# Layer attention: other places among the eight periods of a step for the small operations of each sequence, with queries and keys still evacuated by two VectorE instructions

## The chip, the cores and the metric

The kernel runs as one program on one core of a Trainium2 chip. The metric is the device time of an execution in microseconds (us); the times below are of three executions and of one more that was profiled. Everything is float32 (some operands are read as fp32r, the same bits).

## The reference

The input is 16 sequences of 256 tokens with 128 features. The program computes a four-layer network, a mixture of experts, a second attention and the mixture of experts again. The change is in the attention of the four layers, `_attn`:

```python
for l in range(L):                       # L = 4
    m = _mamba(x, ...)
    x = _ln(x + m, g1[l], be1[l])
    a = _attn(x, W_qkv[l], b_qkv[l], W_ao[l], b_ao[l])
    x = _ln(x + a, g2[l], be2[l])
    h = gelu(x @ W_f1[l].T + b_f1[l]); x = x + h @ W_f2[l].T + b_f2[l]

def _attn(x, W_qkv, b_qkv, W_ao, b_ao):  # 16 heads of 8, per sequence of 256 tokens
    q, k, v = split(x @ W_qkv.T + b_qkv)
    scores = einsum('bhqd,bhkd->bhqk', q, k) * SCALE
    wts = softmax(scores, axis=-1)
    o = einsum('bhqk,bhkd->bhqd', wts, v)
    return o @ W_ao.T + b_ao
```

## The kernel before

Each engine runs its own stream of instructions, written out by hand; semaphores order them. The layer attention (`head_attention`, one function for each engine) is a pipeline over the 16 sequences, a **step** for each: `heads` calls `step(b, r)` for b = 0 to 15 on every engine (r = b mod 4 picks one of four buffers `hqk` and `hvx`). A step has eight **periods** p = 0 to 7, called p0 to p7 here. B counts sequences over all layers. `nth(s, B)` is the count of semaphore s when the work for B is done.

What a period holds on TensorE (`step`, L892):

- rows: scores with the query on the partition, for two heads of a *later* sequence (b+1 in p0 to p3, b+2 in p4 to p7), into PSUM banks 0 and 1 (`row`, L829). They serve only to find each row's maximum. In an even period VectorE reduces both banks in one instruction (`two_maxima`, L1883). In an odd one it reduces bank 0 (`maxima`, L1876), while ScalarE copies bank 1 out (`copy_row`, L1489), which VectorE then reduces from SBUF (`copied_maxima`, L1892). The rows of the next period wait until banks 0 and 1 are free (`freed`).
- scores: with the key on the partition, for two heads of b, into two of the banks 2 to 5 (`score`, L848). ScalarE takes the exponential of both heads in one instruction of 128x1024 (`exps`, L1468).

Around them stand the small operations, once for each sequence. All but `values` and `raw` (bank 6) go through PSUM bank 7, one after another:

- `project_v` (L822), copied out by `lay_v` on VectorE (L1906). Its input is a copy of x that GpSimd makes (`copy_x`, L2331).
- `project_qk` (L816, L817), evacuated by `evac_qk` on VectorE, two instructions (L1900). GpSimd splits the result in two parts (`parts`, L2338 to L2343), SyncE writes it to HBM (`spill`, L579) and reads it back spread over the partitions (`scatter`, L588).
- the maxima of b+1: GpSimd splits them (`split_max`, L2360), TensorE transposes them (`maxima`, L870), ScalarE copies them out (`max_rows`, L1461), and SyncE sends them by two DMAs into two partitions of each head's block of `hqk` (`send_max`, L595), where the scores of step b+1 pick them up. So TensorE's first wait in a step is `pe.wait_ge(hd_mx, every(hd_mx, B))`.
- `values(b, j)` (L861): weights times v for a quarter j of the heads; ScalarE copies the sum out after the last quarter (`raw`, L1474).
- `sums(b)` (L877) spreads the softmax sums; ScalarE makes their reciprocal by Ln and Exp (`reciprocal`, L1480 and L1482), GpSimd multiplies (`divide`, L2350), `out` (L883) projects, and `add_out` on VectorE (L1913) adds to x.

Before the change the small operations of step b stand so. TensorE: p0 `project_v(b+1)`, p1 `values(b-1, 3)`, p2 `project_qk(b+3)`, p3 `values(b, 0)`, p4 `sums(b-1)`, p5 `values(b, 1)` then the transposes of b+1, p6 `values(b, 2)`, p7 `out(b-1)`. Bank 7 has one user at a time, so each of them waits for the one before to have been read out: `sums(b-1)` in p4 waits for hd_q, the end of `evac_qk(b+3)`, which VectorE does at the end of p3.

The loop `heads` runs step 0, three rounds of four steps, and steps 13 to 15 apart, which leave out what has no later sequence (n1, n2, n3: whether b+1, b+2, b+3 exist).

## Time and profile before

| | |
|---|---|
| three executions | 2674.94, 2678.55, 2682.89 us; median 2678.55 |
| the profiled execution | 2679.11 us, of which 2677.4 us from its first to its last instruction |
| TensorE's mean granted clock | 0.908 of full speed |
| busy, share of the span | TensorE 80%, VectorE 62%, ScalarE 60%, GpSimd 26% |
| attention of layer 0, step 0 to the last `values` | 173.0 to 416.0 us; it occurs four times |
| chain that ended last, largest parts | TensorE L829 8%, VectorE L1883 6%, DMA hqk<-hmt 3% |

A busy share is a mean over stages with different limits. The chain that ended last follows the program back from its last instruction, at each step to what released it. "DMA hqk<-hmt" is the sending of the maxima. In the rows, the third number from the end of a stretch is the granted clock of TensorE (1.00 is 2.4 GHz, 0.50 is 1.2 GHz).

### The profile page before, as it was taken

Reading aid. Unit: us, or ns where it says so; the run is one execution under the profiler, and the core shown is the slowest. Engines: PE = TensorE matmul, PEld = TensorE weight load, DVE = VectorE, ACT = ScalarE, POOL = GpSimd, SP = SyncE. Lnnn points to the kernel's source line nnn. Section 1 sums busy time; section 2 is a strip of 40 time slices with the busy share of each in tenths; the row PEclk is TensorE's granted clock in tenths of the full one; section 3 lists DMA queues with packets and bytes.
Section 4 is the critical chain, followed back from the end, with each engine's and each line's share of the span. In section 5 each row is a group of like instructions: output and inputs, shape, how many; then the busy total and the mean of one; then the engine's idle time right before and its main releaser. Section 6 shows DMA issues by size and latency. Waiting matters only on the chain.

```text
span 2677.4 us, 49462 instructions
## 1 busy us (share of the span) xinstructions
PE 2136.1 (80%) x15147; PEld 1401.1 (52%) x15147; DVE 1664.4 (62%) x2491; ACT 1618.9 (60%) x2604; POOL 700.9 (26%) x980
## 2 busy tenths in 40 slices
PE   6968889987888896888899688887877478886795
PEld 4534445643444663444475344454666347775584
DVE  4557775656775765777475577756643267767541
ACT  6447778745777763777784477886544214454461
POOL 0113221022231102223101233211757130004664
PEclk8969999996999997899999699998988789997897
DMA  3033320013331002333000333204141201004223
GB/s 114 10 96 107 110 74 7 9 45 92 110 100 50 16 0 81 94 100 108 20 9 10 96 97 112 81 7 88 46 118 53 70 0 32 1 9 93 79 90 128
DMA packets 116930, 171.73 MB, mean 64 GB/s; under 512 B 13728, under 2 KB 75168, under 8 KB 116512
## 3 DMA queue, kind: packets, MB, share of 16 engines
q1 hardware_dynamic: 107552, 150.66, 19.9%
q0 software_dynamic: 9216, 19.02, 2.0%
q8 instruction: 88, 1.44, 0.2%
q14 instruction: 74, 0.61, 0.1%
HBM read 85.19 MB, written 82.35 MB: 63 GB/s over the span
## 4 chain that ended last, share of the span: by engine, by line
PE 49%; DVE 14%; POOL 11%; issue 10%; DMA 6%; ACT 6%; SPq 1%; DVEq 1%; ACTq 0%; POOLq 0%
PE ps L829 8%; DVE hmx L1883 6%; POOL back_scratch L2420 6%; PE ps L861 5%; POOL slot_scratch L2415 5%; DMA hqk<-hmt 3%; PE ps L877 2%; ACT hrow L1489 2%; PE ps L762 2%; PE ps L726 2%; PE ps L732 2%; PE ps L677 2%; PE ps L683 2%; PE ps L1257 1%; PE ps L1149 1%
## 5 line engine op out<-in xcount | busy, mean ns | idle before, releaser
L1468 ACT ACTIVATE hpt<-ps 128x1024 f32<-128x1024 f32 x512 | 518.5, 1020 | 57.3 <-PE ps L848 56.8
L829 PE MATMUL ps<-hqk 24*128 24x256 f32 x2048 | 287.1, 361 | 154.9 <-DVE hmx L1883 92.0
L829 PEld LDWEIGHTS ps<-hqk 24*128 24x128 f32 x2048 | 173.3, 208 | 368.3 <-DVE hmx L1883 207.6
L1883 DVE TENSOR_REDUCE hmx<-ps 128x4 f32<-128x1024 f32 x256 | 312.8, 1222 | 62.2 <-PE ps L829 60.0
L861 PE MATMUL ps<-hpt,hvx 128*32 128x256 f32 x4096 | 296.2, 410 | 21.8 <-ACT hpt L1468 21.2
L1876 DVE TENSOR_REDUCE hmx<-ps 128x2 f32<-128x512 f32 x256 | 177.3, 693 | 158.9 <-PE ps L829 158.9
L848 PE MATMUL ps<-hqk 26*128 26x256 f32 x2048 | 271.0, 346 | 2.8 <-ACT hpt L1468 1.6
L1489 ACT ACTIVATE hrow<-ps 128x512 f32<-128x512 f32 x256 | 151.9, 593 | 188.1 <-PE ps L829 188.1
L1892 DVE TENSOR_REDUCE hmx<-hrow 128x2 f32<-128x512 f32 x256 | 176.1, 688 | 40.1 <-ACT hrow L1489 29.9
L2420 POOL DMA_INDIRECT back_scratch<-ys,xslot x160 | 153.2, 958 | 86.8 <-issue 47.9
L848 PEld LDWEIGHTS ps<-hqk 26*128 26x128 f32 x2048 | 161.9, 196 | 22.3 <-ACT hpt L1468 16.5
L861 PEld LDWEIGHTS ps<-hpt,hvx 128*32 128x32 f32 x4096 | 111.8, 114 | 115.2 <-ACT hpt L1468 35.0
L2415 POOL DMA_INDIRECT slot_scratch<-xtok,slot_i x128 | 131.6, 1028 | 62.4 <-issue 38.4
L2360 POOL CAST hhl<-hmx 128x32 fp32r<-128x32 f32 x64 | 13.4, 209 | 404.6 <-DVE hmx L1892 404.6
L2312 POOL MEMSET hqk<- 128x1024 f32 x16 | 14.5, 952 | 390.1 <-PE ps L732 390.1
L1740 DVE TENSOR_TENSOR unit<-ps,rstd 128x512 f32<-128x512 f32 x64 | 44.2, 690 | 104.0 <-ACT rstd L1372 103.2
L2350 POOL TENSOR_TENSOR hon<-hraw,hrec 128x512 f32<-128x512 f32 x64 | 81.4, 1271 | 93.3 <-ACT hrec L1482 93.3
L877 PE MATMUL ps<-hraw,spread 128*128 128x512 f32 x128 | 74.1, 662 | 39.3 <-DVE hqk L1900 39.3
L677 PE MATMUL ps<-streams,center 128*128 128x512 f32 (+1 forms) x192 | 96.0, 623 | 9.4 <-SPq L549 5.1
L2331 POOL COPY hxs<-streams 128x256 f32 (+1 forms) x64 | 25.4, 396 | 298.0 <-PE ps L822 273.2
L1439 ACT ACTIVATE hidh<-ps,mw 128x512 fp32r<-128x512 f32 x128 | 89.4, 698 | 19.9 <-PE ps L789 19.9
L683 PE MATMUL ps<-sq,average 128*128 128x512 f32 x192 | 96.4, 601 | 3.6 <-ACT sq L1358 3.3
(326 smaller groups left out, 5342.9 us busy)
## 6 DMA issues: line engine op xcount, KB each, us to landing
hqk_scratch<-hqks SPq DMA_DIRECT2D x64, 768.0 KB, 3.2
hqk<-hqk_scratch SPq DMA_DIRECT2D x256, 192.0 KB
slot_scratch<-filler SPq DMA_DIRECT2D x10, 1040.0 KB, 15.7
xslot<-slot_scratch SPq DMA_DIRECT2D x20, 520.0 KB, 4.2
yback<-back_scratch SPq DMA_DIRECT2D x32, 256.0 KB, 4.4
mw<-mw_in SPq DMA_DIRECT2D x10, 516.5 KB, 3.5
w12raw<-w_in SPq DMA_DIRECT2D x1, 2560.0 KB, 9.3
back_scratch<-ys,xslot POOLq DMA_INDIRECT x160, 2.2
```

What stands on the lines that cost most here:

```text
L677: mm(ps[:, k, :], center[:], src[:, ds(c * CH, CH)], start=True, stop=True).then_inc(ln_cen, 1)
L683: mm(ps[:, 4 + k % 2, :], average[:], sq[:, k % 2, :], start=True, stop=True).then_inc(ln_var, 1)
L829: return mm(ps[:, o % 2, qt * SEQ:(qt + 1) * SEQ], hqk[r][32 * g:32 * g + 24, j, 0, qt * P:(qt + 1) * P], hqk[r][32 * g:32 * g + 24, j, 1, ...
L848: return mm(ps[:, 2 + g, kt * SEQ:(kt + 1) * SEQ], hqk[r][32 * g:32 * g + 26, j, 1, kt * P:(kt + 1) * P], hqk[r][32 * g:32 * g + 26, j, 0, ...
L861: last = mm(ps[32 * g:32 * g + 32, 6, (j // 2) * SEQ:(j // 2 + 1) * SEQ], hvx[r][:, kt, g, j, :], hpt[:, j, g, kt, :], start=j % 2 + kt == ...
L1468: A(hpt[:, j, g:g + 2, :, :], ps[:, 2 + g:4 + g, :], ACT.Exp, scale=QSCALE).then_inc(hd_exp, 1)
L1489: A(hrow[:, o // 4 % 2].rearrange("p t k -> p (t k)"), ps[:, 1, :], ACT.Copy).then_inc(hd_max[1], 1)
L1876: V.tensor_reduce(hmx[:, r, :, 4 * g + j], ps[:, o % 2, :].rearrange("p (t k) -> p t k", t=2), AX.X, ALU.max).then_inc(hd_max[0], 1)
L1883: V.tensor_reduce(hmx[:, r].rearrange("p t (g j) -> p g t j", j=4)[:, g:g + 2, :, j], ps[:, bank:bank + 2, :].rearrange("p x (t k) -> p x ...
L1892: V.tensor_reduce(hmx[:, r, :, 4 * g + j], hrow[:, o // 4 % 2], AX.X, ALU.max).then_inc(hd_red, 1)
L2415: G_.indirect_dma_start(slot_d, bass.IndirectOffsetOnAxis(slot_i[:, c, t:t + 1], 0), xtok[c][:, t, :], None).then_inc(sent, 16)
L2420: G_.indirect_dma_start(back_d, bass.IndirectOffsetOnAxis(xslot[:, g * 4 + b, D:D + 1].bitcast(I32), 0), ys[:, g % 4, b, :], None).then_in ...
```

## The change

The small operations get other periods. On TensorE: p0 `project_qk(b+3)`, p1 `values(b-1, 3)`, p2 `out(b-2)`, p3 `values(b, 0)`, p4 `sums(b-1)`, p5 the transposes of b+1 then `values(b, 1)`, p6 `project_v(b+1)`, p7 `values(b, 2)`. The waits for bank 7 follow the new order. `out` and `divide` now run a step later (b-2 in place of b-1), so the last two steps hold two of them, and steps 0 and 1 none. VectorE evacuates, lays out and adds in the periods of its producers (p0, p6, p2). ScalarE copies the maxima (`max_rows`) ahead of the exponentials of p5 instead of behind them, and its reciprocal is in two parts: Ln behind the exponentials of p4 (`logarithm`), Exp behind those of p7. GpSimd's order in a step is `divide`, `parts`, `split_max`, `copy_x` in place of `copy_x`, `split_max`, `parts`, `divide`. SyncE's order is as before. The loop has two rounds of four steps, with the others written out. No instruction of a whole step is added or taken away.

```diff
--- before.py
+++ after.py
@@ -526,10 +526,14 @@
 
         def heads(eng, step, last):
 
-            step(0, 0, first=True)
-            with eng.Fori(0, 3) as i:
+            step(0, 0, first=True, second=True)
+            step(1, 1, second=True)
+            with eng.Fori(0, 2) as i:
                 for k in range(4):
-                    step(i * 4 + (1 + k), (1 + k) % 4)
+                    step(i * 4 + (2 + k), (2 + k) % 4)
+            step(10, 2)
+            step(11, 3)
+            step(12, 0)
             step(13, 1, n3=False)
             step(14, 2, n2=False, n3=False)
             step(15, 3, n1=False, n2=False, n3=False)
@@ -595,7 +599,7 @@
                         sp.dma_start(hqk[r][24 + part:P:32, :, 0].bitcast(F32),
                                      hmt[16 * part:16 * part + 16].bitcast(F32)).then_inc(hd_mx, 16)
 
-                def step(b, r, first=False, n1=True, n2=True, n3=True):
+                def step(b, r, first=False, second=False, n1=True, n2=True, n3=True):
                     if n3:
                         spill(b + 3)
                     if n1:
@@ -889,7 +893,7 @@
                         last = mm(ps[:, 7, 0:1], T("wo", x * D, D), T("bv", x, 1), start=x == 0, stop=x == 1)
                     last.then_inc(hd_bp, 1)
 
-                def step(b, r, first=False, n1=True, n2=True, n3=True):
+                def step(b, r, first=False, second=False, n1=True, n2=True, n3=True):
                     B = l * BATCH + b
                     for p in range(8):
                         if p == 0:
@@ -911,41 +915,44 @@
                             last = score(2 * p + 1, r, t)
                         last.then_inc(hd_sc, 1)
 
-                        if p == 0 and n1:
-                            pe.wait_ge(hd_mt, nth(hd_mt, B))
-                            pe.wait_ge(hd_ao, nth(hd_ao, B - 2))
-                            project_v(b + 1)
+                        if p == 0 and n3:
+                            if first:
+                                pe.wait_ge(hd_mt, nth(hd_mt, B))
+                            else:
+                                pe.wait_ge(hd_v, nth(hd_v, B))
+                            project_qk(b + 3)
                         if p == 1 and not first:
                             values(b - 1, 3, (r + 3) % 4)
-                        if p == 2 and n3:
-                            pe.wait_ge(hd_v, nth(hd_v, B + 1))
-                            project_qk(b + 3)
+                        if p == 2 and not second:
+                            if n3:
+                                pe.wait_ge(hd_q, nth(hd_q, B + 3, 1))
+                            else:
+                                pe.wait_ge(hd_v, nth(hd_v, B))
+                            out(b - 2)
                         if p == 3:
                             values(b, 0, r)
                         if p == 4 and not first:
-                            if n3:
+                            if second:
                                 pe.wait_ge(hd_q, nth(hd_q, B + 3, 1))
-                            elif n1:
-                                pe.wait_ge(hd_v, nth(hd_v, B + 1))
                             else:
                                 pe.wait_ge(hd_ao, nth(hd_ao, B - 2))
                             sums(b - 1)
                         if p == 5:
-                            values(b, 1, r)
                             if n1:
                                 if first:
                                     pe.wait_ge(hd_q, nth(hd_q, B + 3, 1))
                                 else:
                                     pe.wait_ge(hd_ln, nth(hd_ln, B - 1))
                                 maxima(b + 1)
-                        if p == 6:
+                            values(b, 1, r)
+                        if p == 6 and n1:
+                            pe.wait_ge(hd_mt, nth(hd_mt, B + 1))
+                            project_v(b + 1)
+                        if p == 7:
                             values(b, 2, r)
-                        if p == 7 and not first:
-                            if n1:
-                                pe.wait_ge(hd_mt, nth(hd_mt, B + 1))
-                            else:
+                            if not n1:
                                 pe.wait_ge(hd_ln, nth(hd_ln, B - 1))
-                            out(b - 1)
+                                out(b - 1)
 
                 def last():
                     values(15, 3, 3)
@@ -1473,11 +1480,14 @@
                     act.wait_ge(hd_on, nth(hd_on, B - 1))
                     A(hraw[:].rearrange("p x n -> p (x n)"), ps[:, 6, :], ACT.Copy).then_inc(hd_raw, 1)
 
-                def reciprocal(b):
+                def logarithm(b):
                     B = l * BATCH + b
                     act.wait_ge(hd_sel, nth(hd_sel, B))
                     act.wait_ge(hd_on, nth(hd_on, B - 1))
                     A(hrec[:].rearrange("p x n -> p (x n)"), ps[:, 7, :], ACT.Ln).then_inc(hd_ln, 1)
+
+                def reciprocal(b):
+                    B = l * BATCH + b
                     act.wait_ge(hd_ln, nth(hd_ln, B))
                     A(hrec[:], hrec[:], ACT.Exp, scale=-1.0).then_inc(hd_rec, 1)
 
@@ -1488,18 +1498,22 @@
                     act.wait_ge(hd_red, nth(hd_red, B, o // 4 - 2))
                     A(hrow[:, o // 4 % 2].rearrange("p t k -> p (t k)"), ps[:, 1, :], ACT.Copy).then_inc(hd_max[1], 1)
 
-                def step(b, r, first=False, n1=True, n2=True, n3=True):
+                def step(b, r, first=False, second=False, n1=True, n2=True, n3=True):
                     for p in range(8):
                         ahead, o = (1, 8 + 2 * p) if p < 4 else (2, 2 * p - 8)
                         if p % 2 == 1 and (n1 if p < 4 else n2):
                             copy_row(b + ahead, o + 1)
+                        if p == 5 and n1:
+                            max_rows(b + 1)
                         exps(b, p)
                         if p == 1 and not first:
                             raw(b - 1)
                         if p == 4 and not first:
+                            logarithm(b - 1)
+                            if not n1:
+                                reciprocal(b - 1)
+                        if p == 7 and not first and n1:
                             reciprocal(b - 1)
-                        if p == 5 and n1:
-                            max_rows(b + 1)
 
                 def first_v():
                     act.wait_ge(pool_step, cleared(l))
@@ -1507,8 +1521,12 @@
 
                 if part == "begin":
                     return [lambda: evac_qk(0), first_v, lambda: evac_qk(1)]
+                def last_reciprocal():
+                    logarithm(15)
+                    reciprocal(15)
+
                 if part == "end":
-                    return [lambda: reciprocal(15)]
+                    return [last_reciprocal]
 
                 evac_qk(2)
                 copy_row(0, 3)
@@ -1913,7 +1931,7 @@
                     V.scalar_tensor_tensor(xa[:, ds(b * SEQ, SEQ)], ps[:, 7, 0:SEQ], hbo[:],
                                            xa[:, ds(b * SEQ, SEQ)], ALU.add, ALU.add).then_inc(hd_ao, 1)
 
-                def step(b, r, first=False, n1=True, n2=True, n3=True):
+                def step(b, r, first=False, second=False, n1=True, n2=True, n3=True):
                     for p in range(8):
                         ahead, o, ra = (1, 8 + 2 * p, (r + 1) % 4) if p < 4 else (2, 2 * p - 8, (r + 2) % 4)
                         if n1 if p < 4 else n2:
@@ -1922,11 +1940,13 @@
                             else:
                                 maxima(b + ahead, o, ra)
                                 copied_maxima(b + ahead, o + 1, ra)
-                        if p == 0 and n1:
+                        if p == 0 and n3:
+                            evac_qk(b + 3)
+                        if p == 2 and not second:
+                            add_out(b - 2)
+                        if p == 6 and n1:
                             lay_v(b + 1, (r + 1) % 4)
-                        if p == 3 and n3:
-                            evac_qk(b + 3)
-                        if p == 7 and not first:
+                        if p == 7 and not n1:
                             add_out(b - 1)
 
                 if part == "end":
@@ -2362,14 +2382,16 @@
                     G_.tensor_tensor(hhl[:, :, 1, :], hmx[:, r], hhl[:, :, 0, :].bitcast(F32), ALU.subtract)\
                       .then_inc(hd_mlo, 1)
 
-                def step(b, r, first=False, n1=True, n2=True, n3=True):
+                def step(b, r, first=False, second=False, n1=True, n2=True, n3=True):
+                    if not second:
+                        divide(b - 2)
+                    if n3:
+                        parts(b + 3)
+                    if n1:
+                        split_max(b + 1, (r + 1) % 4)
                     if n2:
                         copy_x(b + 2)
-                    if n1:
-                        split_max(b + 1, (r + 1) % 4)
-                    if n3:
-                        parts(b + 3)
-                    if not first:
+                    if not n1:
                         divide(b - 1)
 
                 pool.wait_ge(ln_aff, nth(ln_aff, l * (2 * NC)))
```

How the instructions stand now. TensorE, from the rows and scores of p4 to those of p6 in a step inside the loop (829/833 rows, 848/852 scores, 877/881 `sums`, 861/865 `values`, 870/874 transposes; the second number of each is the line after the change). Before:

```order
L877 MATMUL ps<-hraw,spread 128x512
L835 REGISTER_ALU
L829 MATMUL ps<-hqk_161 128x256 x2
L848 MATMUL ps<-hqk_163 128x256 x2
L829 MATMUL ps<-hqk_161 128x256 x2
L848 MATMUL ps<-hqk_163 128x256 x2
L861 MATMUL ps<-hpt,hvx_167 32x256 x8
L870 MATMUL ps<-ident,hhl 32x128 x2
```

The same place after:

```order
L881 MATMUL ps<-hraw,spread 128x512
L839 REGISTER_ALU
L833 MATMUL ps<-hqk_161 128x256 x2
L852 MATMUL ps<-hqk_163 128x256 x2
L833 MATMUL ps<-hqk_161 128x256 x2
L852 MATMUL ps<-hqk_163 128x256 x2
L872 REGISTER_ALU
L874 MATMUL ps<-ident,hhl 32x128 x2
L865 MATMUL ps<-hpt,hvx_167 32x256 x8
```

The transposes have moved from behind the matmuls of `values(b, 1)` to ahead of them.

ScalarE, from the exponentials of p4 to those of p6 (1468/1475 exponentials, 1480/1487 Ln, 1482/1492 Exp of the reciprocal, 1489/1499 `copy_row`, 1461/1468 `max_rows`). Before:

```order
L1468 ACTIVATE hpt<-ps 128x1024
L1478 REGISTER_ALU
L1480 ACTIVATE hrec<-ps 128x512
L1482 ACTIVATE hrec<-hrec 128x512
L1487 ISA
L1488 ISA
L1489 ACTIVATE hrow<-ps 128x512
L1466 REGISTER_ALU
L1468 ACTIVATE hpt<-ps 128x1024
L1459 REGISTER_ALU
L1460 ISA
L1461 ACTIVATE hmt<-ps 32x256
```

The same place after:

```order
L1475 ACTIVATE hpt<-ps 128x1024
L1485 REGISTER_ALU
L1487 ACTIVATE hrec<-ps 128x512
L1497 ISA
L1498 ISA
L1499 ACTIVATE hrow<-ps 128x512
L1466 REGISTER_ALU
L1467 ISA
L1468 ACTIVATE hmt<-ps 32x256
L1473 REGISTER_ALU
L1475 ACTIVATE hpt<-ps 128x1024
```

The Exp of the reciprocal has left this place, and `max_rows` stands ahead of the exponentials of p5.

VectorE, from the maxima of p3 to those of p4 (1892/1910 `copied_maxima`, 1883/1901 `two_maxima`, 1900/1918 `evac_qk`). Before:

```order
L1892 TENSOR_REDUCE hmx<-hrow 128x2
L1897 ISA
L1898 REGISTER_ALU
L1900 TENSOR_SCALAR hqk_169<-ps,tw 128x256 x2
L1882 ISA
L1883 TENSOR_REDUCE hmx<-ps 128x2x2
```

After, where the two evacuations stand now, between the maxima of p0 and those of p1 (1894 is `maxima`):

```order
L1901 TENSOR_REDUCE hmx<-ps 128x2x2
L1915 ISA
L1916 REGISTER_ALU
L1918 TENSOR_SCALAR hqk_169<-ps,tw 128x256 x2
L1893 REGISTER_ALU
L1894 TENSOR_REDUCE hmx<-ps 128x2
```

The pair of evacuations has moved from ahead of the `two_maxima` of p4 to ahead of the `maxima` of p1.

## Rows read from the trace of the kernel before

**Rows 1.** Stretches: length, busy us of PE, PEld, DVE, ACT, POOL, clock, DMA

```profile
173.03:191.67 18.64, 15.41 (x122) 8.06 (x123) 11.54 (x16) 9.71 (x13) 3.43 (x7) 0.50 0.17 61
314.25:330.42 16.17, 13.57 (x146) 7.18 (x146) 11.67 (x17) 11.88 (x17) 4.68 (x8) 0.89 0.33 99
345.30:360.19 14.89, 12.12 (x145) 6.39 (x145) 11.75 (x17) 11.73 (x17) 4.67 (x8) 1.00 0.36 108
316.00:318.00 2.00, 1.90 (x24) 0.81 (x24) 1.68 (x4) 1.25 (x2) 0.06 (x1) 0.71 0.80 169
1658.00:1660.00 2.00, 2.00 (x26) 0.84 (x24) 1.38 (x2) 1.57 (x3) 0.00 (x0) 0.57 0.81 169
```

**Rows 2.** Timeline of TensorE in one step: start us, us, [idle before <-releaser]

```profile
345.30 0.38 PE L829 MATMUL ps<-hqk 24*128 24x256 f32 x2 [0.51 <-DMA hqk<-hmt]
...
345.74 0.71 PE L822 MATMUL ps<-tw,hxs 128*128 128x128 f32 x4
347.15 0.38 PE L829 MATMUL ps<-hqk 24*128 24x256 f32 x2 [0.69 <-DVE hmx L1883]
...
348.58 0.38 PE L829 MATMUL ps<-hqk 24*128 24x256 f32 x2
...
350.43 0.38 PE L829 MATMUL ps<-hqk 24*128 24x256 f32 x2 [0.28 <-DVE hmx L1883]
...
351.87 0.38 PE L829 MATMUL ps<-hqk 24*128 24x256 f32 x2
...
353.23 1.12 PE L877 MATMUL ps<-hraw,spread 128*128 128x512 f32 x2 [0.86 <-DVE hqk L1900]
354.36 0.39 PE L829 MATMUL ps<-hqk 24*128 24x256 f32 x2
...
355.81 0.39 PE L870 MATMUL ps<-ident,hhl 128*32 128x128 f32 x2
356.19 0.38 PE L829 MATMUL ps<-hqk 24*128 24x256 f32 x2
...
357.11 1.07 PE L861 MATMUL ps<-hpt,hvx 128*32 128x256 f32 x16 [0.41 <-ACT hpt L1468]
358.11 0.38 PE L829 MATMUL ps<-hqk 24*128 24x256 f32 x2
...
358.54 1.13 PE L883 MATMUL ps<-hon,tw 128*128 128x256 f32 x4
```

**Rows 3.** Timeline of VectorE in the same step

```profile
345.87 1.23 DVE L1883 TENSOR_REDUCE hmx<-ps 128x4 f32<-128x1024 f32 x1 [0.29 <-PE ps L829]
347.01 0.41 DVE L1906 COPY hvx<-ps 128x256 f32<-128x256 f32 x1
...
352.31 0.87 DVE L1900 TENSOR_SCALAR hqk<-ps,tw 128x256 f32<-128x256 f32 x2
353.09 1.22 DVE L1883 TENSOR_REDUCE hmx<-ps 128x4 f32<-128x1024 f32 x1
```

**Rows 4.** Timeline of ScalarE in the same step

```profile
347.79 0.60 ACT L1489 ACTIVATE hrow<-ps 128x512 f32<-128x512 f32 x1 [0.78 <-PE ps L829]
...
354.39 0.60 ACT L1480 ACTIVATE hrec<-ps 128x512 f32<-128x512 f32 x1 [0.82 <-PE ps L877]
355.02 0.63 ACT L1482 ACTIVATE hrec<-hrec 128x512 f32<-128x512 f32 x1
...
356.94 0.36 ACT L1461 ACTIVATE hmt<-ps 32x256 fp32r<-32x256 f32 x1
```

**Rows 5.** Timeline of GpSimd in the same step

```profile
353.44 0.61 POOL L2338 CAST hqks<-hqk 128x512 fp32r<-128x512 f32 x1 [0.35 <-DVE hqk L1900]
...
356.06 1.27 POOL L2350 TENSOR_TENSOR hon<-hraw,hrec 128x512 f32<-128x512 f32 x1
```

**Rows 6.** The chain that ended last, between two steps: start us, us, what

```profile
357.32 0.55 SPq L595
...
357.91 1.97 DMA hqk<-hmt
```

## The prediction

> **What bounds the kernel now.** I read the list of waits first, then the chain that ended last, then one step of layer 0 on each engine, and last the granted clock of several stretches. In the steps at full clock no engine is full: of 14.89 us TensorE is busy 12.12, VectorE 11.75, ScalarE 11.73 [rows 1]. The step is held by a chain that goes to and fro. TensorE writes rows, VectorE or ScalarE must empty banks 0 and 1, and only then may the next rows come. The reader is to see in the timeline how long each period lasts, from one row of L829 to the next [rows 2]: p0 1.85, p1 1.43, p2 1.85, p3 1.44, p4 2.49, p5 1.83, p6 1.92, and p7 to the end of the step at 360.19 [rows 1] 2.08 us.
>
> Two of these lengths are natural. In an even period VectorE starts its double reduction 0.57 after the rows (345.87 against 345.30), it takes 1.23 [rows 3], and TensorE goes on about 0.05 later: 1.85. TensorE's own work fits under it: rows and scores take 0.44 (345.30 to 345.74), and the `project_qk` of p2 ended 0.28 before p3 began, so at 1.57 [rows 2]. In an odd period with `values` TensorE is busy throughout: 0.44 and about 1.0, that is 1.43. The copy by ScalarE there starts at 0.64 and ends at 1.24 [rows 4], so it is hidden.
>
> The rest is stall, at three places [rows 2]. In p4 `sums` stood idle 0.86 for the evacuation of queries and keys, and it ended only at 354.35: 2.49 in place of 1.85. In p6 `values(b, 2)` waited 0.41 for exponentials that ScalarE did late, since Ln and Exp stood ahead of them [rows 4]: 1.92 in place of 1.85. In p7 `out` takes no longer than `values`, but the next step waited 0.51 for the maxima to arrive (the bracket of the first row shows this at the start of this step): 2.08 in place of 1.43.
>
> **The change, part by part.**
>
> *Evacuation out of p3.* The two instructions hold VectorE 0.78 (352.31 to 353.09) ahead of p4's double reduction [rows 3]. In the new order p4's `sums` waits for `add_out(b-2)` of p2, which is long over. It starts at 0.44 and ends at 1.57, under the 1.85 of the period. Gain 2.49 - 1.85 = 0.64.
>
> *Evacuation into p0.* `project_qk` there ends at 1.57. VectorE is free for its next instruction 1.14 after the start of its reduction (347.01 against 345.87), at 0.57 + 1.14 = 1.71. The pair occupies it to 2.49. The rows of p1, which starts at 1.85, are ready for VectorE some 0.53 later, at 2.38: the `maxima` of p1 starts 0.11 late, at 2.49, and with 0.69 (an estimate: somewhat over half of the double reduction's 1.22) ends at 3.18. TensorE is held by `values` until 1.85 + 1.43 = 3.28. Cost nothing, with 0.05 to 0.1 to spare. This is the tightest place, and the one where two instructions in place of one would show. If the cover is gone, each 0.1 of lateness costs 0.1 a step.
>
> *Maxima earlier.* Now the transposes are issued at 0.44 of p5 and take 0.38 (355.81 to 356.19). ScalarE copies bank 1 at 0.64, is free again 0.48 later, and does `max_rows` from about 1.12 to 1.48 of p5. Before, it ended at 357.30, which is 2.94 into p5. Behind it stay the same two issues, one of 0.55, and the transfer of 1.97 [rows 6]: from 357.30 to TensorE's start at 360.19 are 2.89. So the maxima arrive at 1.48 + 2.89 = 4.37 after the start of p5. The step ends at 1.83 + 1.85 + 1.43 = 5.11. The wait is gone with 0.74 to spare. Gain in p7 2.08 - 1.43 = 0.65. What is behind `send_max` on SyncE's queue, `scatter(b+3)`, starts earlier too and harms nothing. `spill(b+3)`, ahead of it, hangs on `parts`, which start some 3 us into the step and last 2.62 (353.44 to 356.06) [rows 5]: done near 5.5, long before `send_max` at about 10.
>
> *Ln in p4, Exp behind p7.* `sums` ends at 1.57, Ln takes 0.60 [rows 4], so it ends at about 2.2 of p4; the transposes need bank 7 at 1.85 + 0.44 = 2.29. It fits by less than 0.1. Behind the transposes on TensorE `values(b, 1)` and all rows of p6 are queued, so lateness here would be paid in full. The exponentials of p5 start at 1.38 of p5 and end at 2.4; their user `values(b, 2)` now stands in p7, at 1.83 + 1.85 + 0.44 = 4.12. The wait in p6 is gone. p6 has `project_v`, 0.71 [rows 2], under VectorE's 1.85: gain 1.92 - 1.85 = 0.07. The Exp (0.63) follows p7's exponentials and pushes those of the next p0 by 0.4, to end near 2.2; ScalarE's next work, the copy of p1, comes at 1.85 + 0.64 = 2.49. GpSimd's `divide`, 1.27 [rows 5], ends near 2.5 of the next step, and `raw` in p1 needs it at 3.9, `out(b-2)` in p2 at 3.28 + 0.44 = 3.72. Here 1.2 are to spare. The ends of Exp, raw and `divide` are late next, but nobody waits.
>
> *Order of the same instructions:* p5 keeps 1.83, whichever of transposes and `values` is first. More written-out steps in place of a round of the loop: I take nothing, as no back-jump shows as a stall in TensorE's timeline.
>
> **The sum.** A whole step at full clock becomes 4 x 1.85 + 3 x 1.43 + 1.83 = 13.52, against 14.89: 1.36 less (0.64 + 0.65 + 0.07). Steps 2 to 12 of a layer have this, 11 x 1.36 = 15.0. Step 0 runs at half clock, 18.64 [rows 1], where TensorE is the bound nearly throughout; the same matmuls in another order give nothing. Step 1 comes to full clock in its middle: 0.9, an estimate from p4 to p7. Step 13 has no `project_qk`, so no wait in p4 to lose: 0.72. At the end an `out` and a `divide` more in step 15, where ScalarE's exponentials are the bound: I take a loss of 0.2 (bounds +0.2 and -1.1, a full `out`). Together 15.0 + 0.9 + 0.72 - 0.2 = 16.4 a layer, 65.7 for four.
>
> *The clock.* A step in which the clock falls lasts 16.17, 1.28 more [rows 1]. I counted eight short falls in steps 2 to 12 of the four layers, from the one at 316 to the one at 1658 [rows 1], each just behind the thin stretch of p7 and p0, where TensorE stands still twice. These gaps are filled now (`project_qk` in p0), and the thinnest place is p6. The Trainium skill, TensorE: Matmul & The Clock Gate, Part 1, says that activity releases the clock and idleness takes it back; by it, with no long idleness in a step, there would be no falls, before or after, and nothing to gain: 2613. The trace does not agree: it has falls with TensorE never idle longer than 0.9 in the step. I take half of the eight falls away: 4 x 1.28 = 5.1. The bounds are all eight (10.2) and eight more (-10.2).
>
> The sum against the profiled execution's own 2679.11: 2679.1 - 65.7 - 5.1 = 2608. The median of the runs, 2678.55, is 0.02% away, so it holds for the median as well.
>
> **The rivals.**
> (a) Part of the stall comes back at a tight place: Ln to transposes, or evacuation to `maxima` of p1, each with 0.1 or less to spare. With 0.5 a step given back (half an exponential on ScalarE), 52 steps x 0.5 = 26: 2634. For it: both margins are as small as the 0.1 to which I can read starts. Against it: what I used are gaps between starts in the same step. Chance 0.17.
> (b) The clock falls no longer: 2603. Denser work in p7 and p0 speaks for it, falls of unclear origin against. Chance 0.2; it lies in the likeliest one's range.
> (c) Slower: the clock. At half clock a step takes 18.6 or more [rows 1], 5.1 above the new 13.52, since TensorE has nothing to hide it under. The gain of 1.36 is used up when TensorE is at half clock for 1.36/5.1 = 27% of steps 1 to 12; before, the eight falls cost 8 x 1.28, as much as 2.7 steps of the 44 at half clock (each 18.64 - 14.89 = 3.75), 6%. If the half clock of step 0 and 1 lasted five steps longer in each layer, 20 x 5.1 - 65 = +37: 2716. Nothing in the order asks for it; the pattern of the first two steps is only slightly changed. Chance 0.04.
> (d) The change does not do what it says, as another wait takes the whole 1.36: a late Ln by 1.4 would, and so would `send_max` held back behind `spill` by over 0.74 + 1.4. Then 2679. Chance 0.03.
>
> **How the numbers follow.** The forecast has 0.56, with (b) as its lower edge 0.76: 2596 to 2625. (a) reaches to 2645. I give 2592 to 2640. A measurement of this kernel can tell about 0.3% (8 us) from no change. Forecast, (b) and (a) are faster by more than that: 0.93; within it (d) and little of (c): 0.035; slower 0.035.
>
> **What would show it.** In the changed kernel's trace: a step of 13.5 at full clock; no wait of L833 for DMA hqk<-hmt and none of `sums` for the evacuation; `max_rows` starting within 1.2 of p5's rows; even periods of 1.85 and odd ones of 1.43; `maxima` of p1 starting about 0.1 behind its rows. Steps 14 and 15 unchanged in length to 0.5. The prediction is wrong if even periods are longer than 1.9 (VectorE late), if the transposes wait for Ln, or if the mean granted clock falls below 0.88.

## The result

The changed kernel takes 2605.3 us (median of four, 2592.7 to 2607.8), the kernel before 2680.7 in the same comparison (2674.9 to 2686.4). The ratio is 0.971, with a 95% interval of 0.967 to 0.975. Forecast were 2608 us and a range of 2592 to 2640.

| | before | after |
|---|---|---|
| the profiled execution, its span | 2679.1, 2677.4 | 2607.8, 2606.1 |
| a steady step at full clock | 14.88 | 13.53 |
| 11 steps, from `sums(1)` to `sums(12)`, four layers | 665.3 | 595.0 |
| steps among them in which the clock fell, apart from a fall that begins in the last 0.7 | 8 | 0 |
| from the first scores of a layer to `sums(1)`, four layers | 175.2 | 167.0 |
| from `sums(12)` to `sums(15)`, four layers | 144.5 | 146.4 |
| TensorE's mean granted clock | 0.908 | 0.906 |

The span is 71.3 shorter, and the eleven steady steps of four layers hold 70.3 of it. These are the stretches of the four layers before and after, from the view of chosen stretches; the columns are as in [rows 1]. Before:

```profile
217.17:382.39 165.22, 134.08 (x1580) 70.51 (x1581) 128.52 (x174) 128.62 (x176) 50.95 (x86) 0.99 0.36 108
664.43:832.06 167.63, 136.83 (x1580) 71.75 (x1580) 128.23 (x174) 128.68 (x176) 50.94 (x86) 0.97 0.36 106
...
sum 665.34, PE 541.37 PEld 284.33 DVE 513.24 ACT 514.31 POOL 203.73; mean PE 135.34 PEld 71.08 DVE 128.31 ACT 128.58 POOL 50.93
```

And after, the same view:

```profile
217.13:365.89 148.76, 130.71 (x1584) 69.48 (x1580) 129.22 (x175) 128.05 (x177) 49.37 (x84) 1.00 0.40 118
645.66:794.41 148.75, 130.70 (x1584) 69.48 (x1580) 129.21 (x175) 128.04 (x177) 49.33 (x84) 1.00 0.40 118
...
sum 595.01, PE 522.85 PEld 277.96 DVE 516.87 ACT 512.18 POOL 197.39; mean PE 130.71 PEld 69.49 DVE 129.22 ACT 128.05 POOL 49.35
```

The reader is to see that the busy time of VectorE and ScalarE hardly changed. What went is mostly TensorE's waiting (665.3 less 541.4 busy before, 595.0 less 522.9 after, so 124 against 72), and the clock is 1.00 in every layer. Of the 70.3, 44 x (14.88 - 13.52) = 59.8 are shorter steps, and 10.5 the falls of the clock that no longer occur. (14.88 stands for the usual step; at full clock single ones of the 44 took 13.97 to 15.60 before, and 13.48 to 13.54 after.) The mean clock of the whole execution is no higher for it: the stretches at half clock outside these steps stay, in a shorter execution, and two falls are new there (below).

One step after the change on TensorE, from its timeline, which answers to [rows 2]. It begins at 304.79; the rows above that are p5, p6 and p7 of the step before it.

```profile
299.70 0.39 PE L833 MATMUL ps<-hqk 24*128 24x256 f32 x2 [0.28 <-DVE hmx L1901]
...
300.18 0.39 PE L874 MATMUL ps<-ident,hhl 128*32 128x128 f32 x2
300.50 1.07 PE L865 MATMUL ps<-hpt,hvx 128*32 128x256 f32 x16
301.50 0.38 PE L833 MATMUL ps<-hqk 24*128 24x256 f32 x2
...
303.35 0.38 PE L833 MATMUL ps<-hqk 24*128 24x256 f32 x2 [0.70 <-DVE hmx L1901]
...
304.79 0.38 PE L833 MATMUL ps<-hqk 24*128 24x256 f32 x2
...
306.64 0.39 PE L833 MATMUL ps<-hqk 24*128 24x256 f32 x2 [0.28 <-DVE hmx L1901]
...
308.10 0.39 PE L833 MATMUL ps<-hqk 24*128 24x256 f32 x2
...
309.95 0.38 PE L833 MATMUL ps<-hqk 24*128 24x256 f32 x2 [0.28 <-DVE hmx L1901]
...
311.39 0.38 PE L833 MATMUL ps<-hqk 24*128 24x256 f32 x2
```

The periods last: p5 1.80, p6 1.85, p7 1.44, p0 1.85, p1 1.46, p2 1.85, p3 1.44. Every idle time left is VectorE's double reduction, in an even period. No row of the step waits for a DMA or for `evac_qk`. VectorE's timeline of the same stretch, which answers to [rows 3]:

```profile
305.36 1.23 DVE L1901 TENSOR_REDUCE hmx<-ps 128x4 f32<-128x1024 f32 x1
306.50 0.87 DVE L1918 TENSOR_SCALAR hqk<-ps,tw 128x256 f32<-128x256 f32 x2
307.29 0.68 DVE L1894 TENSOR_REDUCE hmx<-ps 128x2 f32<-128x512 f32 x1
```

ScalarE's, which answers to [rows 4]:

```profile
300.36 0.60 ACT L1499 ACTIVATE hrow<-ps 128x512 f32<-128x512 f32 x1 [0.30 <-PE ps L833]
300.85 0.36 ACT L1468 ACTIVATE hmt<-ps 32x256 fp32r<-32x256 f32 x1
```

And SyncE's queue, which answers to [rows 6]:

```profile
301.23 1.11 SPq L599 DMA_DIRECT2D hqk<-hmt  x2
302.57 1.55 SPq L592 DMA_DIRECT2D hqk<-hqk_scratch  x4
310.42 0.35 SPq L583 DMA_DIRECT2D hqk_scratch<-hqks  x1
```

The evacuation starts 1.71 into the step and the `maxima` of p1 2.50, as worked out (1.71, 2.49). `max_rows` starts 1.15 into p5 and ends at 1.51 (1.12, 1.48). The spill is issued 5.6 into the step. The maxima are issued 4.3 behind the spill of their own step, at 301.23 in a step that began 13.53 before 304.79, so 10.0 into it.

### The profile page after: what moved, and what is told of

Read it like the earlier page. It is cut to its first block, busy times and chain, and to the rows that moved or that the text cites. A ratio compares the mean times of both kernels' runs of the same rounds, so it can differ in the third digit from the quotient of the medians.

```text
span 2606.1 us, 49174 instructions
## 1 busy us (share of the span) xinstructions
PE 2120.5 (81%) x15147; PEld 1396.0 (54%) x15147; DVE 1667.8 (64%) x2491; ACT 1613.6 (62%) x2604; POOL 703.9 (27%) x980
## 4 chain that ended last, share of the span: by engine, by line
PE 57%; DVE 18%; POOL 10%; issue 8%; ACT 3%; DMA 3%; DVEq 1%; SPq 1%; ACTq 0%; POOLq 0%
DVE hmx L1901 12%; PE ps L833 11%; PE ps L865 10%; POOL slot_scratch L2437 5%; POOL back_scratch L2442 4%; PE ps L766 2%; PE ps L730 2%; PE ps L736 2%; PE ps L681 2%; PE ps L687 2%; PE ps L1264 1%; PE ps L1241 1%; PE ps L1156 1%; PE ps L1189 1%; PE ps L791 1%
## 5 line engine op out<-in xcount | busy, mean ns | idle before, releaser
L865 PE MATMUL ps<-hpt,hvx 128*32 128x256 f32 x4096 | 290.3, 403 | 0.0
L1910 DVE TENSOR_REDUCE hmx<-hrow 128x2 f32<-128x512 f32 x256 | 176.0, 688 | 10.5
L1866 DVE TENSOR_TENSOR hidl<-hid,hidh 128x1024 fp32r<-128x1024 f32 x64 | 78.4, 1224 | 31.5 <-ACT hid L1447 30.0
L1374 ACT ACTIVATE logv<-ps,acol 128x512 f32<-128x512 f32 x96 | 65.8, 685 | 52.8 <-PE ps L687 52.4
L2351 POOL COPY hxs<-streams 128x256 f32<-128x256 f32 (+1 forms) x64 | 25.5, 398 | 252.3 <-PE ps L826 227.5
## 6 DMA issues: line engine op xcount, KB each, us to landing
slot_scratch<-filler SPq DMA_DIRECT2D x10, 1040.0 KB, 15.6
```

Source lines behind the costliest of these rows:

```text
L865: last = mm(ps[32 * g:32 * g + 32, 6, (j // 2) * SEQ:(j // 2 + 1) * SEQ], hvx[r][:, kt, g, j, :], hpt[:, j, g, kt, :], start=j % 2 + kt == ...
L1910: V.tensor_reduce(hmx[:, r, :, 4 * g + j], hrow[:, o // 4 % 2], AX.X, ALU.max).then_inc(hd_red, 1)
```

## The experiments

Step lengths are intervals between the `sums` of two sequences, read from each kernel's timeline. "b" stands for the kernel before with an edit, "a" for the changed kernel with an edit. The first four kernels ran on a chip on which the kernel before takes 2859 us, 180 more. The kernel before has no profile there, but the four have: from `sums(15)` of layer 4 to the end of the program they take 1091 to 1098, the kernels of the other chips 915 to 919. So the extra time lies behind the attention of the layers, ratios are a little diluted by it, and I go by step lengths and by the 44 steady steps as well. These are the 44 steady steps of each profiled execution:

| kernel | usual step at full clock | the 44 steps | of them with a fall of the clock |
|---|---|---|---|
| before | 14.89 | 665.3 | 8 |
| b_fill | 14.89 | 655.1 | 0 |
| b_max | 14.89 | 655.1 | 2 |
| b_evac | 14.65 | 689.0 | 24 |
| b_both | 14.67 | 672.2 | 15 |
| changed, changed again | 13.53 | 595.0, 595.1 | 0, 0 |
| a_undo3 | 13.85 | 614.8 | 3 |
| a_parts | 14.67 | 733.6 | 38 |
| a_parts_sp | 15.02 | 696.6 | 27 |
| a_evac4 | 13.78 | 614.2 | 3 |
| a_evac1 | 13.52 | 594.7 | 0 |
| a_rec | 13.53 | 596.9 | 1 |
| a_split | 13.21 | 587.8 | 3 |

### Evacuation alone: b_evac

```diff
-                        if p == 3 and n3:
+                        if p == 2 and n3:
                             evac_qk(b + 3)
```

> The kernel before with one edit: VectorE evacuates queries and keys at the end of p2, right behind its double reduction, in place of the end of p3. Theory of three separate stalls: the wait of sums in p4 goes, p4 falls from 2.49 to 1.85 us, a step from 14.89 to 14.25, 12 steps in each of 4 layers: 31 us less than before (2648). The pair ends 0.1 late for the maxima of p3, hidden under values. Rival, one chain through the arrival of the maxima: the maxima of the next sequence arrive later relative to the step and p7 grows by as much as p4 loses, 2679. Second rival, that the gain comes mostly from the clock falling less often: step lengths at full clock unchanged.

Measured 2888.9 against 2859.1: ratio 1.0125 (1.009 to 1.016), slower. Single steps at full clock take mostly 14.4 to 14.9, usually 14.65: 0.24 less than before, where 0.64 was forecast. What makes the kernel slower is the clock: the 44 steady steps took 689.0, with mean clocks of 0.87 to 0.97 in the four layers. p4 lost its wait as expected (its `sums` start behind the scores at once), but p7 grew. SyncE's timeline between two steps:

```profile
298.98 0.35 SPq L579 DMA_DIRECT2D hqk_scratch<-hqks  x1
299.43 1.67 SPq L595 DMA_DIRECT2D hqk<-hmt  x2
```

ScalarE's, the copy that makes the maxima ready:

```profile
299.05 0.36 ACT L1461 ACTIVATE hmt<-ps 32x256 fp32r<-32x256 f32 x1
```

The chain, with the transfer of the maxima:

```profile
300.02 2.61 DMA hqk<-hmt
```

And TensorE's timeline, the matmul that waits for it:

```profile
302.94 0.38 PE L829 MATMUL ps<-hqk 24*128 24x256 f32 x2 [1.01 <-DMA hqk<-hmt]
```

The maxima were ready at 299.41, 0.43 behind the start of the spill's issue. The two issues took 1.67 in place of 1.11 and the transfer 2.61 in place of 1.97 [rows 6]. The wait at the end of p7 doubled. The size of the spill, from the page of the kernel before, with the number of transfers, their size and the time from issue to landing:

```profile
hqk_scratch<-hqks SPq DMA_DIRECT2D x64, 768.0 KB, 3.2
```

My theory of separate stalls fell here. The first rival had the mechanism, a chain through the arrival of the maxima, but p7 grew by less than p4 lost.

### Maxima alone: b_max, and both: b_both

```diff
                         if p == 5:
-                            values(b, 1, r)
                             if n1:
                                 ...
                                 maxima(b + 1)
+                            values(b, 1, r)
```

```diff
+                        if p == 5 and n1:
+                            max_rows(b + 1)
                         exps(b, p)
                         ...
-                        if p == 5 and n1:
-                            max_rows(b + 1)
```

> The kernel before with the transposes of p5 ahead of values(b, 1) on TensorE, and max_rows ahead of the exponentials of p5 on ScalarE. Theory: the maxima leave about 0.9 us earlier, the wait of 0.5 for their arrival goes. But the exponentials of p5 are 0.26 later and values(b, 2) in p6 waits for them longer, so the step falls by only 0.38, from 14.89 to 14.5: 20 us less (2660). Rival, that the arrival is the only thing that holds p6 to p0: a step falls by 0.65, 34 us less (2646).

Measured ratio 0.996 (0.9945 to 0.998). Steady steps take 14.8 to 15.1, as before; on the mean of the 44 a step is 0.05 shorter, and not 0.38. Most of the 7.5 us gained is the clock: 2 of the 44 steps have a fall, where the profile of the kernel before, on another chip, has 8. The transposes, now first, waited for Ln (0.18), which still stood behind `sums` held up by the evacuation, and the sending ran into the spill. TensorE's timeline:

```profile
293.89 0.39 PE L870 MATMUL ps<-ident,hhl 128*32 128x128 f32 x2 [0.18 <-ACT hrec L1480]
```

SyncE's timeline:

```profile
295.06 0.35 SPq L579 DMA_DIRECT2D hqk_scratch<-hqks  x1
295.45 1.71 SPq L595 DMA_DIRECT2D hqk<-hmt  x2
```

> The two edits together: evacuation behind the double reduction of p2, and transposes and max_rows first in p5. Theory of separate stalls: the gains add up, step 13.87 (14.89 - 0.64 - 0.38), 51 us less than before (2628), which leaves 0.35 a step to the changed kernel, for values(b, 2) waiting in p6. Rival, one chain: together no more than the larger of the two.

Measured ratio 1.0035 (1.0015 to 1.0054), steps at full clock mostly 14.2 to 14.8, the 44 steps 672.2. The maxima were ready at 294.24, but SyncE sends in order: the spill went out at 294.72 and they at 295.11, and their transfer took 2.67. The gains do not add up. In the kernel before, these two edits bring nothing while the spill keeps its place; the two with an earlier spill were not tried.

### Three parts put back: a_undo3

```diff
                             logarithm(b - 1)
-                            if not n1:
-                                reciprocal(b - 1)
-                        if p == 7 and not first and n1:
-                            reciprocal(b - 1)
+                            reciprocal(b - 1)
```

and the two edits of b_max undone.

> The changed kernel with three of its parts put back as before: the Exp of the reciprocal right behind Ln in p4, transposes behind values(b, 1), max_rows behind the exponentials of p5. Theory: max_rows ends at about 2.65 of p5 in place of 1.5, the maxima arrive 2.89 later at 5.54, the step would have ended at 5.11 of p5: 0.43 a step, 52 steps, 22 us above the changed kernel's 2605 (2627). Rival, that the order of ScalarE does not matter once bank 7 has its new order: 2605. On the clock: if the stall between p7 and p0 is what lets it fall, short falls come back in steps 2 to 12.

Steps of 13.85, 0.32 above the changed kernel (0.43 forecast), the ratio to before 0.979 (0.977 to 0.982). TensorE waited some 0.3 for the maxima between p7 and p0. Of the eleven steady intervals of a layer only the last, up to `sums(12)`, showed a fall of the clock, in three of the four layers.

### The spill back beside the maxima: a_parts and a_parts_sp

```diff
                     if not second:
                         divide(b - 2)
-                    if n3:
-                        parts(b + 3)
                     if n1:
                         split_max(b + 1, (r + 1) % 4)
+                    if n3:
+                        parts(b + 3)
```

> The changed kernel with one line order undone on GpSimd: split_max ahead of parts. So the spill of queries and keys, which SyncE issues ahead of send_max, leaves at about 10.5 us of a step in place of 5.6, just before the maxima at 9.9. Theory from the first four runs, collision: where the spill was issued right before send_max (kernels b_evac, b_both), the two issues of send_max lasted 1.7 in place of 1.11 and the transfer 2.6 in place of 1.97. Then the maxima arrive at about 10.5 + 0.4 + 0.6 + 2.6 + 0.3 = 14.4, 0.85 behind the step's 13.53: 44 us above the changed kernel, step 14.4. And the clock falls often, since TensorE waits 0.9 between p7 and p0. Rival, that only bank 7's order counts: step 13.53 and about 2.9% below before, as the changed kernel.

Ratio 1.028 (1.025 to 1.031): slower than before, and 5.9% above the changed kernel, by the place of one operation of GpSimd. ScalarE's timeline, the copy that makes the maxima ready:

```profile
314.89 0.36 ACT L1468 ACTIVATE hmt<-ps 32x256 fp32r<-32x256 f32 x1
```

SyncE's timeline:

```profile
316.01 0.35 SPq L583 DMA_DIRECT2D hqk_scratch<-hqks  x1
316.40 1.72 SPq L599 DMA_DIRECT2D hqk<-hmt  x2
```

The chain, a microsecond on:

```profile
316.99 2.67 DMA hqk<-hmt
```

TensorE's timeline, one step earlier:

```profile
305.31 0.39 PE L833 MATMUL ps<-hqk 24*128 24x256 f32 x2 [1.06 <-DMA hqk<-hmt]
```

Two things delay the maxima here. They are ready at 315.25, but stand behind the spill in SyncE's order, and the spill waits for `parts` until 316.01: they are issued at 316.40, 1.15 later than they could be. Then the transfer takes 2.67 in place of 1.97, 0.70 more. Less the 0.74 that the prediction had to spare, that makes a wait of 1.1, and 1.06 is what TensorE shows. So more than half of the delay is the order on the queue, and the rest the transfer that runs beside the spill.

At full clock, as in the first layer, single steps are mostly 14.6 to 14.8 (14.4 forecast). In the other three layers the clock fell in nearly every step, and steps took 17.1. Stretches of the steady steps, first layer and third:

```profile
217.25:388.25 171.00, 141.52 (x1585) 74.75 (x1581) 129.56 (x175) 130.04 (x177) 51.93 (x89) 0.93 0.35 104
...
1134.86:1322.58 187.72, 163.00 (x1584) 86.51 (x1581) 129.62 (x175) 131.62 (x177) 51.87 (x88) 0.80 0.32 95
```

The same kernel and the same work, 171 or 188 us by the clock. So the late maxima cost about 1.1 a step, and the clock that falls with them twice that.

In a_parts_sp SyncE sends the maxima first as well:

```diff
-                    if n3:
-                        spill(b + 3)
                     if n1:
                         send_max(b + 1, (r + 1) % 4)
+                    if n3:
+                        spill(b + 3)
```

> As the kernel with split_max ahead of parts, and SyncE issues send_max ahead of the spill. If the spill in front of the maxima is the cause, the maxima leave alone and the step returns to 13.53; the scatter behind the spill is late by some 3 us, and may now reach p4 of the next step late by up to 0.5 (step 14.0). If the lateness comes from GpSimd itself, the step stays at 14.4.

Ratio 1.008 (1.005 to 1.011), steps of 14.6 to 17.0 at full clock and up to 19.4 with a fall. The wait for the maxima is gone. But the spill is late now, and what follows it reaches p4 too late. The chain, two steps of it:

```profile
299.09 3.23 DMA hqk_scratch<-hqks
...
303.60 5.61 DMA hqk<-hqk_scratch
```

TensorE's timeline where it waits for such a transfer:

```profile
309.44 0.38 PE L833 MATMUL ps<-hqk 24*128 24x256 f32 x2 [1.53 <-DMA hqk<-hqk_scratch]
```

I had expected up to 0.5 for this; in the steady steps it is mostly 1.0 to 2.0, and up to 3.5. So the total does not show what the maxima alone gain by this order. The spill must leave early in the step: both for the maxima and for itself.

### Margins: a_evac4, a_evac1, a_rec

a_evac4 splits each evacuation in two of 128 columns:

```diff
-                        V.tensor_scalar(hqk32[:, a, :], ps[:, 7, a * SEQ:(a + 1) * SEQ], T(bias), None, ALU.add)\
-                         .then_inc(hd_q, 1)
+                        for h in range(2):
+                            last = V.tensor_scalar(hqk32[:, a, h * P:(h + 1) * P],
+                                                   ps[:, 7, a * SEQ + h * P:a * SEQ + (h + 1) * P], T(bias), None, ALU.add)
+                        last.then_inc(hd_q, 1)
```

> The changed kernel with queries and keys evacuated by four VectorE instructions of 128 columns in place of two of 256. Theory, that p1 has no margin: the four occupy about 1.04 in place of 0.78, the maxima of p1 start 0.26 later, TensorE's p2 waits for them: 0.25 a step, 13 us above the changed kernel, step 13.78. Rival, a margin of some tenths that the steady step does not show: 13.53.

Steps of 13.78, to the hundredth as forecast: p1 has no margin. The ratio to before is 0.978 (0.976 to 0.980); 2623.9 us are 18 above the changed kernel on the same chip (2605.9, below), where 13 were forecast. In three layers the clock fell at the end of the 44 steps.

a_evac1 uses one instruction:

```diff
-                    for a, bias in enumerate(("bq", "bk")):
-                        V.tensor_scalar(...).then_inc(hd_q, 1)
+                    V.tensor_tensor(hqk32[:], ps[:, 7, :].rearrange("p (a n) -> p a n", a=2),
+                                    T("bq", 0, 2).unsqueeze(2).broadcast_to([P, 2, SEQ]), ALU.add).then_inc(hd_q, 2)
```

> The changed kernel with queries and keys evacuated by one VectorE instruction of 512 columns (bias broadcast) in place of two. Theory from the four-instruction kernel, where each tenth more was paid: below two there is 0.03 left before values bounds p1, so 13.50, 1 to 2 us less, not to be told from the changed kernel. Rival: one instruction saves 0.1 to 0.2 a step, 5 to 10 us.

Steps of 13.52, 2607.9 against 2605.9 for the changed kernel on the same chip: no difference. Two instructions are as good as one.

a_rec has the Exp of the reciprocal back in p4, the first diff of a_undo3 alone:

> The changed kernel with the Exp of the reciprocal back behind Ln in p4. Theory: ScalarE's copy of p5 and max_rows are 0.25 later, the maxima arrive at about 4.65 of p5, still ahead of the step's end at 5.11: 13.53, the same time. So setting Exp apart is worth nothing by itself in the new order. Rival: it carries the 0.3 a step that the kernel with three parts put back lost, 17 us.

Steps of 13.53, 2600.5 against 2605.9, ratios to before 0.9685 (0.966 to 0.971) and 0.970 (0.968 to 0.973): not to be told apart. Setting Exp apart brought nothing.

### The clock: b_fill

```diff
                             pe.wait_ge(hd_ao, nth(hd_ao, B - 2))
+                            mm(ps[:, 7, SEQ:CH], T("wv"), xa[:, ds(b * SEQ, SEQ)], start=True, stop=True)
                             project_v(b + 1)
```

> The kernel before with one matmul of 128x256 more in p0, ahead of project_v, into columns of bank 7 that nobody reads: work that computes nothing, in the 0.69 us that TensorE waits for VectorE there. Theory, that the thin stretch of p7 and p0 lets the clock fall: step unchanged at 14.89 at full clock, fewer falls than the 8 in steps 2 to 12, up to 10 us less than before (0.4%). Rival, that falls come from something else: the same number of falls, the same time or 1 to 2 us more.

Ratio 0.994 (0.992 to 0.996): a kernel with more work is faster. Steps are as long as the full-clock ones of the kernel before (14.86 to 15.07, except that the first of a layer's eleven takes 15.4 to 15.6 and the last 14.0), and none of the 44 has a fall. The stretches of the first two layers, which answer to those of before shown above:

```profile
216.73:380.44 163.71, 137.06 (x1602) 73.86 (x1602) 128.22 (x174) 128.19 (x176) 50.95 (x86) 1.00 0.37 109
660.20:824.07 163.87, 137.00 (x1603) 73.88 (x1603) 128.25 (x174) 128.17 (x176) 50.96 (x86) 1.00 0.36 108
...
sum 655.13, PE 548.00 PEld 295.44 DVE 512.99 ACT 512.65 POOL 203.79; mean PE 137.00 PEld 73.86 DVE 128.25 ACT 128.16 POOL 50.95
```

665.3 less 655.1 is 10.2, the eight falls of 1.28. The other executions bear it out: the mean granted clock of the six of b_fill is 0.912 to 0.919, that of the eleven of the kernel before in the same comparison 0.902 to 0.911. Filling a gap elsewhere in the step was not tried.

### The changed kernel again, and a version that goes further: after_again, a_split

> The changed kernel again, on the same chip as the next three. Steps of 13.53, 2.9% below before.

2605.9, ratio 0.970 (0.968 to 0.973), steps of 13.53.

a_split halves two of the `values`, to put a half each into even periods, where TensorE waits for VectorE:

```diff
                         if p == 4 and not first:
                             ...
                             sums(b - 1)
+                        if p == 4:
+                            values(b, 1, r, (0,))
                         if p == 5:
                             ...
-                            values(b, 1, r)
+                            values(b, 1, r, (1,))
                         if p == 6 and n1:
                             ...
                             project_v(b + 1)
+                        if p == 6:
+                            values(b, 2, r, (0,))
                         if p == 7:
-                            values(b, 2, r)
+                            values(b, 2, r, (1,))
```

> The changed kernel with values(b, 1) and values(b, 2) in halves of eight matmuls: the first half of values(b, 1) behind sums in p4, the first half of values(b, 2) behind project_v in p6. Theory: even periods are held by VectorE (1.85) with TensorE idle 0.3 in p4 and 0.7 in p6, odd ones by TensorE. p4 grows to 2.07, p5 falls from 1.83 to 1.33, p7 from 1.43 to 1.29: step 13.1, 0.42 less, 22 us below the changed kernel (0.8%). The maxima arrive at 4.37 of p5, the step ends at 4.47. Rival, ScalarE is full by then (11.7 busy of 13.1) and its lateness gives the gain back: 13.5.

2590.8, ratio to before 0.966 (0.964 to 0.9685), steps of 13.20, the fastest kernel. On TensorE, the starts of p5, p6, p7 and p0:

```profile
296.26 0.39 PE L833 MATMUL ps<-hqk 24*128 24x256 f32 x2
...
297.62 0.38 PE L833 MATMUL ps<-hqk 24*128 24x256 f32 x2
...
299.47 0.38 PE L833 MATMUL ps<-hqk 24*128 24x256 f32 x2
...
300.83 0.38 PE L833 MATMUL ps<-hqk 24*128 24x256 f32 x2 [0.29 <-ACT hrow L1504]
```

p5 is 1.36 (1.33 forecast), p7 1.36 (1.29); p4 is 2.06. The gain of 0.33 was forecast as 0.42, and 15 us against the changed kernel as 22. The 44 steps show only 7.3 us of it (587.8 against 595.1), since in three layers the clock fell at their end, in step 13. Ratios 0.966 and 0.970 were taken in two comparisons; their intervals touch, and it is the step lengths that tell the two apart.

## Why the prediction was right, and where its working was not

*What bounds the kernel.* Right. The natural lengths of 1.85 and 1.43, and the step made of them, 13.52, were met with 13.48 to 13.54 in all 44 steady steps.

*Evacuation out of p3.* The 0.64 was gained, but taking away the wait of `sums`, as I had put it, is not enough. b_evac takes that wait away and nothing else; its step at full clock is 0.24 shorter, and it is 1.3% slower by the clock. What I called separate stalls were coupled by the spill: where p4 is shorter, the maxima are ready sooner, just as the 768 KB of the spill set out ahead of them on SyncE's queue. The weak step is the sentence on `spill(b+3)`, "long before `send_max`": I had the times (5.5 and about 10), and they were right, but I used them only to show that nothing is harmed. They are what the gain of p7 rests on. a_parts shows it: with the spill back at 10, about 1.1 a step are lost at full clock, most of the 1.36. It is what rival (d) describes, `send_max` held back behind `spill`, to which I gave 0.03 and no connection with the new order of GpSimd that prevents it.

*Evacuation into p0.* Right to 0.03: p1 is 1.46, not 1.43, and a_evac4 paid its 0.25 in full. So the 0.05 to 0.1 that I had to spare there are not there. That two instructions cost nothing against one was shown by a_evac1.

*Maxima earlier.* Arrival before the end of the step: right. Of the two orders that bring it, the exchanges in p5 carry it; with Exp, too, back in p4 they are worth 0.32 (a_undo3), while Exp alone is worth nothing (a_rec). That the exchanges alone, with Exp apart, are worth something was not tried.

*Ln in p4.* It fitted; the transposes started at 0.48 of p5 in place of 0.44. Rival (a) did not occur.

*The clock.* The place was right, the size of the term wrong: I took half of the eight falls away (5.1), all eight went (10.5). Rival (b), which I had given 0.2, is what happened in these steps. b_fill shows that these eight need the idle time in p0: some 0.5 us of matmul work that computes nothing, put into p0 of the old kernel, takes the idle time there from 0.69 to 0.27 and removes all eight falls, though the wait of 0.5 at the end of p7 stays. a_parts and b_evac, with waits of 1.0 to 1.2 at the end of p7, have falls in nearly every or in every second step. The Trainium skill, TensorE: Matmul & The Clock Gate, describes under "A second HAM failure mode" a kernel that cycles through PSUM banks, in which short idle times between groups of matmuls come often enough to make the clock go up and down. This trace agrees: before the eight falls TensorE was never idle longer than 0.94 at a stretch. The rule from Part 1 that the prediction set against the trace does not cover them.

The change also made a new gap, which I had overlooked. In steps 13 and 14 there is no `project_qk`, and `project_v` has moved to p6, so p0 holds nothing but rows and scores. TensorE's timeline of p1 of step 14, in layers 1 and 3:

```profile
374.24 0.38 PE L833 MATMUL ps<-hqk 24*128 24x256 f32 x2 [1.35 <-DVE hmx L1901]
...
1229.30 0.58 PE L833 MATMUL ps<-hqk 24*128 24x256 f32 x2 [1.34 <-DVE hmx L1901]
```

In layers 3 and 4 the clock falls there, in layers 1 and 2 it does not, after the same wait (matmuls of 0.58 in place of 0.38 show it). a_split and a_evac4 have their falls of layers 2 to 4 behind the same gap of step 13. So such gaps go with the falls; which of them brings one, no run explains.

*The other terms.* Steps 0, 1 and 13 and the end of the layer were to give 4 x 1.4 = 5.7, and gave 1.0 together with everything outside. The first steps gave 8.2, more than the 3.6 forecast for step 1. Step 2 begins in that stretch too, and the moment at which the full clock comes back varies: b_fill, with the order of the kernel before, took 171.2 there, 4 less than before. From `sums(12)` on, 1.9 were lost: in layers 3 and 4 the clock fell for some 10 us behind the new gap of step 14, where before it had fallen for 3 to 7 in step 13 of three layers. The term for the `out` and `divide` more in step 15 (0.2 a layer) can't be told from this; only step 15 holds two of them, not the last two steps. The stretch of the third layer:

```profile
1226.00:1240.00 14.00, 12.62 (x102) 6.19 (x102) 7.36 (x10) 9.04 (x12) 1.73 (x3) 0.63 0.00 1
```

The remaining 5.4 were lost where no instruction was changed: 1.6 ahead of the first attention and 6.0 between the attentions, less 2.2 gained behind them. In the profiles of all kernels a stretch between two attentions takes 199 to 205 with the same instructions, and b_fill lost 4.3 of the 6.0 too, so much of it need not come from the change. I did not find the cause; more instructions are loaded (queue q8 has 108 packets, before 88), and that was not tested. So the total of 71.3 against 70.8 forecast is in part luck: the clock term 5.4 too small, the others 4.7 too large.

## What to carry to other kernels

When a pipeline waits at several places in a step, take the step's natural length from what each period needs, and then ask of each transfer not only whether it arrives in time but what leaves on the same queue right ahead of it once the step gets shorter. Removing one wait of several can cost time: here it moved a small urgent transfer right behind a large one, and the clock fell. Where TensorE waited anyway, a matmul that computes nothing was free here, and paid by the clock. And where operations change places, look at the steps that leave some of them out: there the old gap may be open again.

## What the runs showed of the hardware

A transfer of 16 KB on which the step waits took 1.97 us when a transfer of 768 KB had been issued on the same queue 1.1 us ahead, as in the kernel before, and 2.5 to 2.7 when it had been issued about 0.4 to 0.5 us ahead. The two issues took 1.6 to 1.7 in that case, and 1.11 both with 1.1 us between and with the 4.3 of the changed kernel. The Trainium skill, Trainium Kernel Development and Optimization, Key Constraints, says that DMAs issued from the queues of SyncE, ScalarE and GpSimd run on the same 16 engines and interleave. Both transfers here come from one queue, SyncE's; that the small one takes 0.5 to 0.7 longer beside the large one is what the trace shows, and on which engines they meet was not looked into.

TensorE's clock fell from 2.4 to 1.2 GHz in eight steady steps of the kernel before, where TensorE was busy 81% of the time and not idle longer than 0.94 us at a stretch before the fall. With 0.5 of idle at the end of p7 and 0.7 in p0, 8 of 44 steps had a fall; with these 0.7 brought down to 0.3, none; with 1.0 to 1.2 at the end of p7, 24 to 38 of 44 (b_evac, a_parts). In a_split, busy 92% of the steady steps, the falls stand behind the one gap of 1.3 us in step 13.

Four kernels ran on a chip where the kernel before takes 2859 us, 6.7% more than on the others. The profiles put 172 to 182 us of it behind the attention of layer 4, with a mean granted clock of 0.81 there against 0.88 on the other chips. Why that chip is slower there, no run shows.
